# A GAT layer on one core: layer 1's spread rows as bf16 products of three parts, and a new order of TensorE, VectorE and ScalarE around them

## The reference

```python
xl = (x @ W).reshape(n, heads, out_ch)
alpha_src = jnp.einsum('nhc,hc->nh', xl, a_src)
alpha_dst = jnp.einsum('nhc,hc->nh', xl, a_dst)
e = jax.nn.leaky_relu(alpha_src[src] + alpha_dst[dst], 0.2)
m = jax.ops.segment_max(e, dst, num_segments=n)
e = jnp.exp(e - m[dst])
s = jax.ops.segment_sum(e, dst, num_segments=n)
alpha = e / (s[dst] + 1e-16)
out = jax.ops.segment_sum(xl[src] * alpha[:, :, None], dst, num_segments=n)
h = relu(layer_norm(out + bias)) + (h0 @ Wr1 + br1)
```

## Time and profile before

| | |
|---|---|
| median of 3 runs | 1156.68 us (1153.5 to 1158.72) |
| the profiled execution's own time | 1156.89 us |
| span of its trace | 1155.2 us |
| PE busy | 1079.0 us (93%) |
| DVE busy | 697.0 us (60%) |
| ACT busy | 357.9 us (31%) |
| POOL busy | 139.1 us (12%) |
| mean granted TensorE clock | 0.977 |

### The profile page before, as it was taken

One profiled execution on the slowest core, in us unless ns is written; L12 is line 12 of the kernel. 1 busy time (PEld: TensorE's weight loads), 2 busy tenths in 40 slices (PEclk: granted clock), 3 DMA queues, 4 the chain that ended last, 5 costly groups with the idle time before them and its releaser, 6 DMA issues.

```text
span 1155.2 us, 15235 instructions
## 1 busy us (share of the span) xinstructions
PE 1079.0 (93%) x4473; PEld 719.5 (62%) x4474; DVE 697.0 (60%) x1682; ACT 357.9 (31%) x628; POOL 139.1 (12%) x262
## 2 busy tenths in 40 slices
PE   5999999999899999999999999999996888998994
PEld 3467777665488888855556556656664544654662
DVE  5988889369467767879565416767775532223222
ACT  1222221143377777611001023820000222323331
POOL 3000000000000000011010000102221312323332
PEclk9999999999999999999999998999998799998998
DMA  9535555611134101062122100333445855374333
GB/s 249 186 129 206 200 201 171 221 37 38 42 114 157 48 1 37 0 194 85 50 66 62 38 17 27 88 142 100 116 121 202 286 187 181 130 269 161 133 100 106
DMA packets 53566, 141.45 MB, mean 122 GB/s; under 512 B 8345, under 2 KB 17081, under 8 KB 53249
## 3 DMA queue, kind: packets, MB, share of 16 engines
q1 hardware_dynamic: 42321, 109.17, 28.5%
q0 software_dynamic: 8160, 23.16, 6.2%
q10 hardware_dynamic: 3024, 8.36, 2.4%
HBM read 81.89 MB, written 61.48 MB: 124 GB/s over the span
## 4 chain that ended last, share of the span: by engine, by line
PE 41%; issue 38%; DVE 9%; DMA 6%; DVEq 2%; SPq 1%; POOL 1%; ACT 0%; ACTq 0%; POOLq 0%
PE PSA L1777 10%; PE PSA L1727 9%; PE PSA L1716 7%; PE PSA L1836 5%; PE PSA L1850 5%; DMA RX<-out,RX 3%; DVE RW2X L852 2%; DMA out<-RX 2%; DVE RB L866 1%; DVE RW2X L854 1%; DVE RK L786 1%; PE PSA L1821 1%; DVEq L844 1%; PE PSA L1798 1%; DVEq L852 1%
## 5 line engine op out<-in xcount | busy, mean ns | idle before, releaser
L1700 PE MATMUL PSA<-RW2X 125*125 125x257 f32 x800 | 175.6, 383 | 3.8 <-DVE RW2X L917 3.8
L1700 PEld LDWEIGHTS PSA<-RW2X 125*125 125x125 f32 x800 | 150.9, 189 | 28.9 <-issue 4.6
L1777 PE MATMUL PSA<-RW2X,RW 125*125 125x385 f32 (+1 forms) x360 | 124.1, 495 | 0.0
L1836 PE MATMUL PSA<-RW2X,RX 128*128 x276 | 101.1, 518 | 11.6 <-ACT RX L1443 7.6
L1538 PE MATMUL PSA<-RW,RX 128*125 128x512 f32 x240 | 108.3, 602 | 1.9 <-ACT RX L1256 1.9
L1555 PE MATMUL PSA<-RW,RX 128*125 128x512 f32 (+2 forms) x360 | 109.5, 458 | 0.0
L1727 PE MATMUL PSA<-RW2X,RX 128*125 128x384 f32 x320 | 108.4, 494 | 1.0 <-DVE RW2X L995 1.0
L1716 PE MATMUL PSA<-RW2X,RX 128*125 128x384 f32 x320 | 105.1, 487 | 2.2 <-ACT RX L1366 1.4
L911 DVE TENSOR_TENSOR RW2X<-RW2X 125x625 f32<-125x625 f32 x80 | 64.8, 811 | 63.4 <-ACT RW2X L1355 63.2
L1355 ACT ACTIVATE RW2X<-RX,RK 125x625 f32<-125x625 f32 x120 | 91.5, 811 | 31.3 <-PE PSA L1700 31.3
L1850 PE MATMUL PSA<-RW2X 128*128 x276 | 93.2, 488 | 2.2 <-DVE RX L1179 1.3
(11 more groups left out here) (320 smaller groups left out, 1293.6 us busy)
## 6 DMA issues: line engine op xcount, KB each, us to landing
xs_d<-RB SPq DMA_DIRECT2D x10, 3108.0 KB, 11.5
RW2X<-in_L_ffn_W SPq DMA_DIRECT2D x16, 1152.0 KB, 8.6
RW2X<-xs_d ACTq DMA_DIRECT2D x21, 388.5 KB
RX<-res_d SPq DMA_DIRECT2D x10, 448.0 KB
RX<-in_x SPq DMA_DIRECT2D x12, 336.0 KB
...
```

What stands on the lines that cost most here:

```text
L1700: last = mm(ps[n % 7][0:TP, 0:XW], ering[:, (p * NT + m) % EBUF, 0, i * TP:(i + 1) * TP], xl[:, m, p // 2, :], start=(m == 0), stop=(m == ...
L1777: last = mm(ps[PAIR[t % 3][c]][0:TP, 0:DW - c], p2[m][:, t * TP:(t + 1) * TP], xl2[:, m, c, 0:DW - c], start=(m == 0), stop=(m == NT - 1))
L1836: last = mm(ps[bank][:, 0:FI], xsT[:, kk, :], wbuf[:, ds(w0 + kk * FI, FI)], start=(kk == 0), stop=(kk == KD - 1))
```

## The change

- **Three exact parts.** VectorE's `split` takes the score columns apart into three numbers of bf16 precision whose sum is the float32 value (six small instructions). TensorE transposes the 120 columns (3 parts by 40) at once (`turn_parts`), ScalarE copies the result as bf16 into `partT`. A spread row is then one bf16 product: the stationary operand is a column of `third`, with ones in three rows of 120, broadcast to 125 columns; the moving operand is `partT`. The same is done for the 20 rows of head 0 at the closing part. GpSimd makes `third` once. Layer 2 keeps its own `spread`.
- **Order between the heads.** Residual 6 stands behind the transpose; then come the rows of head 0, the first mask, and the rows of heads 1 to 3 with a third of residual 7 ahead of each. The second mask stands behind the first third of residual 8, the rest of residual 8 behind it. ScalarE's copies follow.
- **Closing part.** A third of residual 18 stands ahead of the wait for `adm`, a third behind the transpose, and the last behind the rows and the transpose of `adm`. Residual 19 moves to PSUM bank 6. ScalarE copies out residual 18 behind the exponentials of two steps and residual 19 behind those of four; the aggregation waits for residual 18's copy at its start, and for residual 19's from its seventh output on.

```diff
+GS = H * NT
...
+        third_f = k(GS, 3 * GS)
+        third = k(GS // 2, 3 * GS).bitcast(BF16)
...
+        a = carver(RW1[:, H * N + N // 2 + TP:KD * C1])
+        prt = r3(a(3 * GS, TP), 3)
+        part_r = a(GS, TP)
+        part_b = r3(a(GS, TP).bitcast(BF16), 2)
+        partT = a(63).bitcast(BF16)[0:3 * GS, 0:TP]
...
+        def res_bank(n):
+            return 6 if n == 2 * NT - 1 else n % 2
...
+            own.link(g.memset(third_f, 0.0))
+            for i in range(3):
+                own.link(g.affine_select(out=third_f, in_=third_f, compare_op=ALU.not_equal, fill=1.0, base=-GS * i,
+                                         pattern=[[-1, GS]], channel_multiplier=1))
+            g.tensor_copy(third, third_f).then_inc(third_ready, 1)
...
+            def split(col, w):
+
+                b0, b1, r, q0, q1, q2 = (i[:, 0:w].rearrange("p (a t) -> p a t", t=NT) for i in (
+                    part_b[:, 0], part_b[:, 1], part_r, prt[:, 0], prt[:, 1], prt[:, 2]))
+                own.link(v.tensor_copy(b0, col))
+                v.tensor_copy(q0, b0)
+                own.link(v.tensor_tensor(r, col, b0, ALU.subtract))
+                own.link(v.tensor_copy(b1, r))
+                own.link(v.tensor_copy(q1, b1))
+                v.tensor_tensor(q2, r, b1, ALU.subtract).then_inc(parts_ready, 1)
+
             dve.wait_ge(dense_act, 3 * NT)
+            split(as_ad[:, :, 0:H].rearrange("p t h -> p h t"), GS)
...
+            dve.wait_ge(adm_ready, 1)
+            dve.wait_ge(parts_turned, 1)
+            split(adm[:, :, 0, :], 2 * NT)
...
-                s.copy(to[:, j * 512:(j + 1) * 512], ps[j][0:TP, :]).then_inc(res1_kept, 1)
+                s.copy(to[:, j * 512:(j + 1) * 512], ps[res_bank(n)][0:TP, :]).then_inc(res1_kept, 1)
...
-            act.wait_ge(dense_act, 3 * NT)
-            mask(0)
-            res_keep(R0)
-            res_keep(R0 + 1)
-            for h in range(H):
+            def asb_keep(h):
                 for c, (b0, nb) in enumerate(CHUNKS):
                     i = 3 * h + c
                     act.wait_ge(asb_done, i + 1)
                     s.copy(as_bc[:, h, b0 * TP:(b0 + nb) * TP], ps[2 + i % 3][0:TP, 0:nb * TP]).then_inc(asb_kept, 1)
-                if h == 0:
-                    mask(1)
+
+            act.wait_ge(dense_act, 3 * NT)
+            act.wait_ge(parts_turned, 1)
+            s.copy(partT, ps[4][0:3 * GS, 0:TP]).then_inc(partT_ready, 1)
+            mask(0)
+            res_keep(R0)
+            asb_keep(0)
+            mask(1)
+            asb_keep(1)
+            asb_keep(2)
+            res_keep(R0 + 1)
+            asb_keep(3)
...
+            act.wait_ge(parts_turned, 2)
+            s.copy(partT, ps[4][0:3 * GS, 0:TP]).then_inc(partT_ready, 1)
             for c in range(5):
                 rrow_keep(c)
-            res_keep(2 * NT - 2)
             act.wait_ge(adm_turned, 1)
             s.copy(admT, ps[7][0:2 * H * NT, 0:TP]).then_inc(admT_ready, 1)
             for i in range(EBUF):
                 exps(0, i)
-                if i == 0:
-                    res_keep(2 * NT - 1)
+                if i == 1:
+                    res_keep(2 * NT - 2)
+            res_keep(2 * NT - 1)
...
-            def res1(n):
+            def res1(n, k0=0, k1=KD):
                 t, j = divmod(n, 2)
-                if n < 2:
-                    pe.wait_ge(ld_wr1[n], 16)
-                else:
-                    pe.wait_ge(res1_kept, n - 1)
-                if n == R0:
-                    pe.wait_ge(dense_act, 3 * NT)
-                for kk in range(KD):
-                    last = mm(ps[j][0:TP, :], xTt[t][:, kk, :], wr1s[:, kk, j * 512:(j + 1) * 512], start=(kk == 0),
-                              stop=(kk == KD - 1))
-                last.then_inc(res1_done, 1)
+                if k0 == 0:
+                    if n < 2:
+                        pe.wait_ge(ld_wr1[n], 16)
+                    elif n == 2 * NT - 1:
+                        pe.wait_ge(rrow_kept, 5)
+                    else:
+                        pe.wait_ge(res1_kept, n - 1)
+                    if n == R0:
+                        pe.wait_ge(dense_act, 3 * NT)
+                for kk in range(k0, k1):
+                    last = mm(ps[res_bank(n)][0:TP, :], xTt[t][:, kk, :], wr1s[:, kk, j * 512:(j + 1) * 512],
+                              start=(kk == 0), stop=(kk == KD - 1))
+                if k1 == KD:
+                    last.then_inc(res1_done, 1)
...
+            def turn_parts(out):
+                tr(out, prt.rearrange("p a b -> p (a b)"), idt).then_inc(parts_turned, 1)
+
+            def spread_part(out, j):
+                return mm(out, third[:, j:j + 1].to_broadcast([3 * GS, TP]), partT, start=True, stop=True)
...
-            res1(R0)
-            res1(R0 + 1)
-            pe.wait_ge(xt_ready, 2 * NT)
-            pe.wait_ge(hist_kept, NP)
-            pe.wait_ge(lmt_ready, 1)
-            mask_turn(0, LM[0], lmt).then_inc(lm_done, 1)
-            for h in range(H):
+            def spread_head(h):
                 for c, (b0, nb) in enumerate(CHUNKS):
                     i = 3 * h + c
                     if i >= 3:
                         pe.wait_ge(asb_kept, i - 2)
                     for m in range(nb):
-                        last = spread(ps[2 + i % 3][0:TP, m * TP:(m + 1) * TP], as_ad[:, b0 + m, h:h + 1])
+                        last = spread_part(ps[2 + i % 3][0:TP, m * TP:(m + 1) * TP], h * NT + b0 + m)
                     last.then_inc(asb_done, 1)
-            for t in range(1, NT):
+
+            pe.wait_ge(parts_ready, 1)
+            turn_parts(ps[4][0:3 * GS, 0:TP])
+            res1(R0)
+            pe.wait_ge(hist_kept, NP)
+            pe.wait_ge(third_ready, 1)
+            pe.wait_ge(partT_ready, 1)
+            spread_head(0)
+            pe.wait_ge(xt_ready, 2 * NT)
+            pe.wait_ge(lmt_ready, 1)
+            mask_turn(0, LM[0], lmt).then_inc(lm_done, 1)
+            for h in range(1, H):
+                res1(R0 + 1, 2 * h - 2, 2 * h)
+                spread_head(h)
+            res1(R0 + 2, 0, 2)
+            pe.wait_ge(lmt_ready, 2)
+            pe.wait_ge(asb_kept, 3 * H)
+            mask_turn(1, LM[1], lmt).then_inc(lm_done, 1)
+            res1(R0 + 2, 2, KD)
+            for t in range(2, NT):
                 res1(R0 + t + 1)
                 pe.wait_ge(lmt_ready, t + 1)
-                if t == 1:
-                    pe.wait_ge(asb_kept, 3 * H)
-                else:
-                    pe.wait_ge(max_step, H * (t - 1))
+                pe.wait_ge(max_step, H * (t - 1))
                 mask_turn(t, LM[t % 2], lmt).then_inc(lm_done, 1)
...
-                    last = spread(ps[bank][0:TP, n * TP:(n + 1) * TP], adm[:, q, h, half * HT + i:half * HT + i + 1])
+                    last = spread_part(ps[bank][0:TP, n * TP:(n + 1) * TP], q * NT + half * HT + i)
...
+            res1(2 * NT - 2, 0, 2)
             pe.wait_ge(adm_ready, 1)
+            pe.wait_ge(parts_ready, 2)
+            turn_parts(ps[4][0:3 * GS, 0:TP])
+            res1(2 * NT - 2, 2, 4)
+            pe.wait_ge(partT_ready, 2)
             for c in range(5):
-                rrow_turn(0, c)
-            res1(2 * NT - 2)
+                rrow_turn(c)
             pe.wait_ge(rrow_kept, 3)
             tr(ps[7][0:2 * H * NT, 0:TP], adm.rearrange("p q h t -> p (q h t)"), idt).then_inc(adm_turned, 1)
+            res1(2 * NT - 2, 4, KD)
             res1(2 * NT - 1)
-            pe.wait_ge(res1_kept, 2 * NT)
+            pe.wait_ge(res1_kept, 2 * NT - 1)
             pe.wait_ge(ones_ready, 1)
             for p in range(PASSES):
                 for m in range(NT):
                     pe.wait_ge(prob_ready, p * NT + m + 1)
                     for i in range(HT):
                         n = HT * p + i
-                        if m == 0 and n in (5, 6):
+                        if m == 0 and n == 5:
                             pe.wait_ge(rrow_kept, 5)
+                        if m == 0 and n == 6:
+                            pe.wait_ge(res1_kept, 2 * NT)
```

More of the change, by code:

```diff
@@ L354, in gnn_ffn @@
         ones_ready = sem("ones_ready")
+        third_ready = sem("third_ready")
+        parts_ready = sem("parts_ready")
+        parts_turned = sem("parts_turned")
+        partT_ready = sem("partT_ready")
         asb_done = sem("asb_done")
@@ L1649, in _, with rrow_turn @@
                     for m in range(nb):
[L1650 removed]
+                        last = spread_part(ps[2 + i % 3][0:TP, m * TP:(m + 1) * TP], h * NT + b0 + m)
                     last.then_inc(asb_done, 1)
[L1652 removed]
+            pe.wait_ge(parts_ready, 1)
[17 more added lines that the diff above has]
+            for t in range(2, NT):
                 res1(R0 + t + 1)
                 pe.wait_ge(lmt_ready, t + 1)
[L1655 to L1658 removed]
+                pe.wait_ge(max_step, H * (t - 1))
                 mask_turn(t, LM[t % 2], lmt).then_inc(lm_done, 1)
             res1(2 * NT - 3)
[L1662 removed]
```

(1 more changed line is left out.)

1 line of the change is left out of this document (removed).

## The result

| | before | changed |
|---|---|---|
| median | 1157.7 us (4 runs, 1153.5 to 1160.42) | 1141.83 us (4 runs, 1140.62 to 1143.95) |
| ratio, 95% interval | | 0.9865 [0.9837, 0.9894] |
| profiled execution | 1156.89 us, span 1155.2 | 1143.95 us, span 1142.1 |
| mean granted TensorE clock | 0.977 | 0.977 |

The changed kernel is 15.9 us faster by the medians (12.9 by the two profiled executions); the interval of the ratio allows for 12.3 to 18.9 us. 1142.5 us were forecast.

A forecast was written before the change was run, and what follows sets the result against it. TensorE was taken as the bound, busy 1079.0 of 1155.2 us. The terms summed to -12.6 us, -14.3 with the clock, from 1156.89 to 1142.6, less 0.2 to the median: 1142.5 us forecast, range 1139.5 to 1147.0.

The forecast's parts named there:

- A row at the mask's pace: The 40 source rows between the heads: each bf16 row takes 0.058 us like a mask product, 2.3 for 9.07 us, -6.7 us.
- Rival B: Spread rows: bf16 rows slower than the mask's products, giving 1145 to 1146 us, or 1151.7 with nothing gained; chance 0.10.
- D: Spread rows: weight load and product do not overlap, about 0.37 us a row, giving 1160.4 us, slower than before; chance 0.02.
- Copies hide between the heads: First part: ScalarE's three copies of a head, 1.32 us, hide behind 2.3 us of TensorE's rows and residual products.
- Split and transpose: Ahead of residual 6: VectorE's six operations end at 220.6 us, TensorE free at 220.45, transpose 0.11 us; +0.2 us.
- Wait for the destination rows: Closing part: TensorE waits 1.2 us for VectorE's second split instead of 1.37; -0.1 us with the second transpose.
- The 20 rows: Closing part's destination rows: held back by ScalarE's copies, 2.0 us for 4.47, so -2.5 us.
- Start of the aggregation: End of the closing part: TensorE no longer waits for step 0's weights, with 1.3 us to spare; -3.8 us.
- The clock: Behind the aggregation's start: with no wait ahead of it, the half-speed stretch in the next 9.84 us goes; -1.7 us.
- The second mask ahead: First part: the earlier second mask gives VectorE slack but leaves the total unchanged; priced at nothing.
- Rival A: Closing part: TensorE's short waits bring the clock down, costing 1.7 to 3.4 us, 1144 to 1146 us; chance 0.28.
- Rival C: Behind the aggregation: later stages waiting for transfers, or other clock drops, give 2 to 5 us back, 1145 to 1148; chance 0.10.

The follow-up runs named there:

- e1_order_f32: Changed kernel with its new order but float32 spread rows, without splits and transposes of the parts: 1150.98 us, ratio 0.9935 to the kernel before.
- e4_no_thirds: Changed kernel with residual 7 whole ahead of the first mask and all four heads' rows in one piece, still bf16: 1149.81 us, ratio 0.9927.
- e3_act_old: Changed kernel with only ScalarE's list of the closing part put back to the old order: 1148.93 us, ratio 0.9921 to the kernel before.
- e2: Changed kernel with the closing part in the old order on TensorE and ScalarE, bf16 rows kept: 1151.83 us, ratio 0.9949 to the kernel before.
- e5_mask_late: Changed kernel with the second mask put back behind the whole of residual 8: 1143.75 us, ratio 0.9858 to the kernel before.
- e0: Changed kernel run once more without any edit: 1143.12 us, ratio 0.9866 to the kernel before.
- e8: Changed kernel with layer 2's 30 spread rows made as bf16 products too: 1141.48 us, ratio 0.9852 to the kernel before.
- e11_best: Changed kernel with layer 2's 30 rows in bf16 and residual 18 in pieces of four, one and one product: 1138.25 us, ratio 0.9824.
- e6_four_ahead: Changed kernel with four of residual 18's six products ahead of the wait for the split, two behind the transpose: 1140.79 us, ratio 0.9853.

## Why the prediction was right, point by point

**The sum.** The stage got 98.71 - 85.41 = 13.3 us shorter and the clock behind it 1.7 us better, 15.0 against 14.3 forecast. The stage beat its part of the sum, 12.6, by 0.7 us, and the list says where. That the median came within 0.7 us of the forecast is in part luck: one more run moved the median of the kernel before from 1156.68 to 1157.7 us. The parts, as far as the runs separate them:

- *A row at the mask's pace, -6.7 us.* Right: 0.058 us each. By the Trainium skill's 81 ns for each product (TensorE: Matmul & The Clock Gate, "Back-to-back issue gap") ten rows would take 0.81 us; the trace has 0.58, so the measurement decides for the row. Rival B is out, and with it D. e1_order_f32, which has no wait at all, shows the whole of the bf16 rows' part as 7.5 us; the sum had -6.7 - 2.5 for the rows, +0.6 for splits, transposes and switches, and 1.2 for the wait that the second split makes, so -7.4. That these agree is in part luck too: without waits a float32 row takes 0.218 us and not the 0.227 that I had, so the rows gain 0.5 us less than priced, and the cheaper splits make up for it.
- *Copies hide between the heads.* Right, and e4_no_thirds shows what it costs when they don't: 4.0 us.
- *Split and transpose.* The transpose started at 223.00, right behind the last product of the counts; the first split cost nothing visible. The sum had 0.2 us for both; they cost 0.13 us, ahead of the stage's start, so the stage is 0.2 of the 0.7 us better.
- *Wait for the destination rows, 1.2 us.* Mis-sized: 0.89 us. The operations on 20 columns start about 0.2 us apart (296.40 to 297.33 for the last of six), not 0.25 to 0.27 as I had from 40 columns, so the split adds 1.1 instead of 1.5 us (297.33 + 0.18 - 296.40). That is 0.3 of the 0.7 us.
- *The 20 rows, 2.0 us.* Right: 2.02.
- *Start of the aggregation, -3.8 us.* Right. The spare time was 1.6 us (1.3 forecast), and e3_act_old shows that without ScalarE's new list all of this gain is gone; the list without TensorE's new order wasn't run. By start times the wait was 3.9 us and not 3.75 (310.10 + 5.15 = 315.25 for the end of residual 19, and 319.16), another 0.16 of the 0.7 us.
- *The clock, -1.7 us.* Right: 1.00 in the 9.84 us behind the start, and 0.83 again in e2 and e3, where the wait is back.
- *The second mask ahead, nothing.* Right, by e5_mask_late: 85.39 against 85.41.

**Four marks that I had set were missed.** The wait ahead of the second transpose was 0.89 us, not 1 to 1.5, as said above. Tile 1's maxima came at 239.44, not about 237, and the aggregation started at 308.54, not 306.5. And a stage behind the aggregation was to begin 13 to 14 us earlier; the first mask of layer 2, before and in the changed kernel, came 11.95 us earlier:

```profile
685.41 0.91 PE L1635 MATMUL PSA<-RK,RW 125*125 125x125 bf16 x12 [1.81 <-ACT RW L1403]
```

```profile
673.46 0.91 PE L1688 MATMUL PSA<-RK,RW 125*125 125x125 bf16 x12 [1.81 <-ACT RW L1446]
```

The last three have one cause in front of the change: in this execution the stage began at 223.13 instead of 220.45. Of these 2.7 us, 1.3 are there when TensorE's second wait for VectorE ends, at 69.32 instead of 68.04 us (the first of the two lasted 1.66 us instead of 0.62); 1.2 are a longer half-speed stretch there (68 to 75 us instead of 68 to 72); 0.13 are the first transpose. GpSimd's first instruction for `third` comes at 143.90, so all but the transpose lies ahead of anything that the change put in. It differs between executions: e5_mask_late, whose program is the same up to there, began the stage at 220.43 and the aggregation at 305.82. It also closes the account of the profiled executions: 15.0 us won in and right behind the stage, 0.7 behind that, 2.7 lost ahead of it, 13.0 of the 13.1 us between the spans. I had worked out the marks as absolute times from one execution, where only the distance from the stage's start is the change's doing. By that distance the maxima are at 16.3 us against 16.5 forecast, the aggregation at 85.4 against 86.1, and layer 2's first mask is 14.6 us earlier.

**Rival A** was the one that could have come true. Its condition, half speed behind the short waits of the closing part, was not met with 0.89 and 0.20 us: in all five traces that show this pair (the changed kernel, e0, e4, e5, e8) what stands behind it ran at full speed. The nearest relative is e4's pair of 0.32 and 1.38 us, with half speed right behind it and 1.6 us lost, the lower end of the price that I had put on A. (The upper end, 3.4 us, took rows 7 over all of 8 us; over TensorE's 7.04 busy ones it is 3.0.) In e2 the clock fell within a single wait of 2.61 us. And the pair of the earlier trace rows, 0.95 and 0.96 us, was not followed by half speed everywhere. In e11_best:

```profile
685.35 0.88 PE L1701 MATMUL PSA<-RK,RW 125*125 125x125 bf16 x12 [0.95 <-DVE RK L1070]
687.18 0.91 PE L1810 MATMUL PSA<-RW2X,RX 128*125 128x384 f32 x2 [0.96 <-DVE RW2X L1035]
684.00:700.00 16.00, 13.54 (x115) 9.43 (x114) 15.69 (x32) 8.97 (x7) 0.00 (x0) 1.00 0.17 49
```

The rule that I had set beside it (the Trainium skill, same page, "A second HAM failure mode: psum-queue depth-cycling") agrees with e4 and with rows 7. But the same waits at the same place left the clock at 1.00 here (and in e6_four_ahead), so the runs don't tell what decides. The falls of e2 and e4 are seen in one trace each.

**Rival C**, a gain given back later, did not happen. From the aggregation's start to the end of the span it was 1155.2 - 319.16 = 836.0 us before and 1142.1 - 308.54 = 833.6 after. Of the 2.4 us, 1.7 are the clock behind the start. The rest is not the clock's (14.0 and 14.3 us were lost to half speed behind 335 us) and wasn't traced.
